# Two moves in a four-stage transformer kernel: where a tile's values are projected, and which engine issues the first stacked queries

## The chip, the cores and the metric

The kernel runs on one core of a Trainium2 chip. The metric is the device time of one execution in microseconds (us). TensorE is called PE here as in the profile, VectorE is DVE, ScalarE is ACT, GpSimd is POOL, and SyncE, which issues most transfers, is SP.

## The reference, cut to what matters

Four blocks follow one another on x of 2048 tokens by 128 channels: an attention with 16 heads of 8 channels over all 2048 keys, a feed-forward block with weights and activations rounded to blockwise FP4, a causal attention over groups of 512 tokens, and a stack of six layers. Each of the six layers is a local attention (16 heads of 64, windows of 32 keys and the window before), an output projection and a feed-forward block:

```
qkv = shift(x) @ Wqkv[i];  q, k, v = split(qkv)          # 128 -> 3 x 1024
q = rotary(l2norm(q) * q_scale);  k = rotary(l2norm(k) * k_scale)
out = softmax(8 * q k^T over the window) @ v;  x = out @ Wo[i] + x
x = (a * gelu(gate)) @ W2[i] + b2 + x,  with a, gate from layernorm(shift(x))
```

## The kernel before

**Start and first attention.** `attention_inputs` normalises x, projects and rotates queries and keys, and cuts each into three bf16 pieces, which SP writes to the DRAM tensor `pieces`. `attentions` follows, after a barrier of all engines. Its SP program loads the pieces back in stacked form: `stack_keys(0, ...)` for the first two pairs of heads (14 transfers), `stack_queries(0, ...)` for the first chunk of 512 queries (12 transfers), `stack_keys(1, ...)` for the other six pairs (14), then `stack_queries` for chunks 1 to 3 (36), then weights. A transfer of `stack_keys` writes 8 partitions with one row of 2048 bf16 elements (4096 bytes) for each pair; one of `stack_queries` writes 8 partitions with eight runs of 512 elements (1024 bytes). All of a core's queues share 16 DMA engines.

The first work of PE is `max_block` of unit 0. It waits for `stack_k[0]` and for `stack_q[0]`, so for all 14 + 12 transfers. DVE reduces each block (`reduce_block`, L914), through a ring of three PSUM banks. Unit 1 waits for `stack_k[1]`, after the 64 blocks of unit 0. Scores, exponentials on ACT and all that comes later follow from there in a fixed order.

**Layers.** `layers` runs 6 layers of 16 tiles of 128 tokens; each engine has its own written-out order of a tile's steps in `attend`, and semaphores tie them. For tile T, PE turns (transposes) the rotated queries of T (`turn` r = 0, 1), does `out_project(T - 2)`, turns the keys (r = 2, 3), projects the keys of T + 1 (`project(l, T + 1, 1, b)`), turns the weights of T - 1, computes `scores(T)` and `values(T - 1)`, projects the queries of T + 2 and last the values of T + 1. The projections of queries and keys share PSUM banks 0 and 1, so each waits until DVE has normalised the one before (`l_qn`, L1656). The values go to banks 3 and 4, which the scores use too: their projection waits for `subtract` of the tile before, and `scores(T)` waits until ACT has copied the values out (`store_values`, L1500). Of the values' copy a shifted one, `V_earlier`, is made by two transfers of SP; `values(T)` waits for them.

ACT stores the turned queries and keys (`store_qk`, L1509 to L1516), squares projected rows for the norms (L1486), moves weights and outputs, takes the exponentials, and ends a tile with `store_values(l, T + 1)`. DVE sums the squares (L1645), normalises (L1656), multiplies by cosines (L1665), and takes maxima, differences and sums of the softmax. POOL makes the sine products and `hat`, the rotated queries (L1209), which `turn` reads.

Of the kernel before, what the change touches and what calls it, by code (L numbers as in the profile page):

```python
# [17 lines left out]
CH = 512  # L18
# [6 lines left out]
HD = P // H  # L25
# [3 lines left out]
TERMS = [(0, 0), (0, 1), (0, 2), (1, 0), (1, 1), (2, 0)]  # L29
# [200 lines left out]
def attentions(nc, t, a, d):  # L230
# [33 lines left out]
    for u in range(causal, NU):  # L264
        width_before.append(width_before[-1] + sum(BLOCK_START + x[3] for x in max_blocks(u)))
    ahead = lambda u: min(start_of(causal) + (first_step[NU - 1] - first_step[causal - 1]) * width_before[u - causal]
                          // width_before[-1], first_step[u] - LEAD)
    for u in range(1, NU):
        blocks = list(enumerate(max_blocks(u)))
        at, until = start_of(u), first_step[u] - LEAD  # L270
        if u >= causal:
            at, until = ahead(u), min(ahead(u + 1) if u + 1 < NU else until, until)
# [43 lines left out]
    with ExitStack() as ctx:  # L316
# [5 lines left out]
        stack_q = [s.stack_q0, s.stack_q1, s.stack_q2, s.stack_q3]  # L322
# [3 lines left out]
        QS = sb("QS", [P, NC, H // 2, CH], BF16)  # L326
# [51 lines left out]
        with nc.Block() as block:  # L378
            @block.sync
            def _(e):  # L380
# [12 lines left out]
                def stack_queries(c, signal):  # L393
                    for odd in range(2):
                        for j in range(len(TERMS)):
                            at = 64 * odd + HD * j
                            e.dma_start(QS[at:at + HD, c, :, :],
                                        paired(d.pieces[0, TERMS[j][0]])[odd][:, :, c * CH:(c + 1) * CH])\
                                .then_inc(signal, 16)
# [44 lines left out]
                        e.dma_start(t.scales[:, 2 * i + 1, ROT:LD], v[:, 0:ROT].partition_broadcast(P)).then_inc(s.w_tab, 16)  # L444

                stack_keys(0, slice(0, 2))
                stack_queries(0, stack_q[0])
                stack_keys(1, slice(2, H // 2))
                for c in range(1, NC):
                    stack_queries(c, stack_q[c])  # L450
# [4 lines left out]
                for u, (A, c, g) in enumerate(units):  # L455
                    e.wait_ge(s.split, 2 * u + 2)
                    for j in range(2):
                        for odd in range(2):
                            at = 64 * odd + MROW + j
# [329 lines left out]

            @block.scalar  # L790
            def _(e):

                def take(use):
                    e.wait_ge(s.st_ready, place[use] + 1)
                    return 2 * pair_of[use]
# [86 lines left out]
                for u, (A, c, g) in enumerate(units):  # L882
                    for kt in range(tiles_of(u)):
                        n = first_step[u] + kt
# [192 lines left out]
def layers(nc, t, a):  # L1077
# [4 lines left out]
    with ExitStack() as ctx:  # L1082
# [47 lines left out]
        with nc.Block() as block:  # L1130
# [115 lines left out]
            def _(e):  # L1246
# [6 lines left out]
                def project(l, T, i, b):  # L1253

                    n = l * NT + T
                    if i == 0 and b == 0 and T % TC == 0:
                        e.wait_ge(s.xs, XS_START + l * SHIFTS - 2 * (NC - 1 - T // TC))
                    if i == 2 and T:
                        e.wait_ge(s.sub, START + n)
                    elif i or T:  # L1260
                        e.wait_ge(s.qn, 2 * (2 * n + i) - 1 + b)
                    if i == 0 and T < 2:
                        e.wait_ge(s.v_done, START + n)
                    at = i * INNER + b * CH
                    e.matmul(ps[:, (V_BANK[T] if i == 2 else 0) + b, :], XS[:, T * P:(T + 1) * P], w_qkv[:, at:at + CH],  # L1265
                             start=True, stop=True).then_inc(s.v_ready if i == 2 else s.a_ready, 1)

                def turn(l, T, r):

                    n = l * NT + T  # L1270
                    i = r // 2
                    e.wait_ge(s.rotated, START + (n * 2 + i) * 3 + 3)
                    if T == 0 and r == 1:
                        e.wait_ge(s.xs, XS_START + l * SHIFTS)
                    if r in (1, 2):
                        e.wait_ge(s.o_free, START + (2 * n - 4 + r if T > 1 else l * (2 * NT)))
                    else:
                        e.wait_ge(s.t_free, START + 4 * n + (1 if r else 0))
                    for j in range(4):
                        at = (4 * (r % 2) + j) * P  # L1280
                        tr = e.transpose(ps[:, TURN_BANK[r], j * P:(j + 1) * P], hat[:, i, at:at + P], t.ident[:, :])  # L1281
                    tr.then_inc(s.t_ready, 1)
# [83 lines left out]
                def attend(l):  # L1366

                    for T in range(NT):
                        ahead = T + 1 < NT
                        turn(l, T, 0)  # L1370
                        turn(l, T, 1)
                        if T >= 2:
                            out_project(l, T - 2)
                        turn(l, T, 2)
                        turn(l, T, 3)
                        if ahead:
                            project(l, T + 1, 1, 0)
                            project(l, T + 1, 1, 1)
                        if T:
                            turn_weights(l, T - 1, 0)  # L1380
                            turn_weights(l, T - 1, 1)
                        scores(l, T, 0)
                        scores(l, T, 1)
                        if T:
                            values(l, T - 1, 0)
                            values(l, T - 1, 1)
                        if T + 2 < NT:
                            project(l, T + 2, 0, 0)
                            project(l, T + 2, 0, 1)
                        if ahead:  # L1390
                            project(l, T + 1, 2, 0)
                            project(l, T + 1, 2, 1)
                    out_project(l, NT - 2)
                    mean(l, 0)
                    mean(l, 1)
                    turn_weights(l, NT - 1, 0)
                    turn_weights(l, NT - 1, 1)
                    values(l, NT - 1, 0)
                    values(l, NT - 1, 1)
                    mean(l, 2)  # L1400
                    out_project(l, NT - 1)
# [74 lines left out]
            def _(e):  # L1476
# [21 lines left out]
                def store_values(l, T):  # L1498
                    e.wait_ge(s.v_ready, START + (l * NT + T) * 2 + 2)
                    e.copy(V[:, T % 3, :], flat2(ps[:, V_BANK[T]:V_BANK[T] + 2, :])).then_inc(s.v_done, 1)  # L1500

                def store_qk(l, T, r):

                    n = l * NT + T
                    e.wait_ge(s.t_ready, START + 4 * n + r + 1)
                    j0 = 4 * (r % 2)
                    if r < 2:
                        bank = ps[:, TURN_BANK[r], :].rearrange("p (j w q) -> p j w q", j=4, q=WIN)
                        e.copy(qT[0:LD, T % 2, j0:j0 + 4, :, 0, :], bank[0:LD, :, :, :])  # L1509
                        e.copy(qT[LD:P, T % 2, j0:j0 + 4, :, 1, :], bank[LD:P, :, :, :]).then_inc(s.t_free, 1)  # L1510
                    else:
                        e.copy(kT[:, T % 2, j0:j0 + 4, WIN:WIN + P], ps[:, TURN_BANK[r], :].rearrange("p (j n) -> p j n", j=4))\
                            .then_inc(s.t_free, 1)
                    if r == 3 and T + 1 < NT:
                        e.wait_ge(s.t_free, START + 4 * n + 4)
                        e.activation(kT[:, (T + 1) % 2, :, 0:WIN], kT[:, T % 2, :, P:P + WIN], ACT.Copy,  # L1516
                                     scale=const[:, 3:4] if (T + 1) % TC == 0 else 1.0)
# [36 lines left out]
                def attend(l):  # L1554
                    for T in range(NT):
                        ahead = T + 1 < NT
                        for r in range(4):
                            store_qk(l, T, r)
                        if ahead:
                            squares(l, T + 1, 1, 0)  # L1560
                            squares(l, T + 1, 1, 1)
                        if T:
                            place_low(l, T - 1, 0)
                        if ahead:
                            inverse_norms(l, T + 1, 1)
                        if T:
                            place_low(l, T - 1, 1)
                        if T:
                            store_o(l, T - 1, 0)
                            store_o(l, T - 1, 1)  # L1570
                        if T + 2 < NT:
                            squares(l, T + 2, 0, 0)
                            squares(l, T + 2, 0, 1)
                        exponentials(l, T)
                        if T + 2 < NT:
                            inverse_norms(l, T + 2, 0)
                        if ahead:
                            store_values(l, T + 1)
                    place_low(l, NT - 1, 0)
                    place_low(l, NT - 1, 1)  # L1580
                    square_centred(l, 0)
                    square_centred(l, 1)
                    store_o(l, NT - 1, 0)
                    store_o(l, NT - 1, 1)
                    square_centred(l, 2)
# [366 lines left out]
```

## Time and profile before

| | |
|---|---|
| median of three runs | 3145.54 us (3144.41 to 3152.8) |
| profiled execution, its own time | 3135.21 us |
| span of the profiled execution | 3133.4 us |
| mean granted PE clock | 0.971 |
| PE, DVE, ACT, POOL busy | 89%, 83%, 71%, 44% of the span |

The span runs from the first to the last instruction of one execution. A busy share is a mean over stages that have different limits, so it doesn't say what a change in one stage is worth. In the timelines the idle time before an instruction and what ended it stand in brackets at the end of a row.

### The profile page before, as it was taken

To read this page: it belongs to the slowest core of one execution; us is meant where nothing else is said; L and a number is where in the kernel's file an instruction comes from. 1 tells how busy PE (TensorE), PEld (TensorE's weight loads), DVE (VectorE), ACT (ScalarE), POOL (GpSimd) and SP (SyncE) were. 2 spreads that over 40 slices of the span, in tenths; PEclk is the share of its full clock that TensorE was granted. 3 is DMA by queue.
4 is the path that set the end of the run, shared out by engine and by line. 5 is a ranking of instruction groups with operands and counts; after the bars stand their busy time and mean duration, and the time that the engine had idled before them with its cause. 6 is when DMAs were issued, how large, how long until landed. Compare 5 with 4: busy or idle time off the path is not lost. (4 is left out here: it accounts for less than half of the span.)

```text
span 3133.4 us, 74866 instructions
## 1 busy us (share of the span) xinstructions
PE 2802.7 (89%) x29085; PEld 1564.2 (50%) x29181; DVE 2594.8 (83%) x3866; ACT 2238.7 (71%) x3690; POOL 1365.0 (44%) x818
## 2 busy tenths in 40 slices
PE   3999898998898989879998998999899899999998
PEld 1233333333333333346655665666476656655764
DVE  4999889888887788469968996998699779968995
ACT  2277777767656667768867886887688778867884
POOL 0200333523335210056645664666466546646661
PEclk8699999999999999989999999999999999999999
DMA  3200001010010020011111111111111111111110
GB/s 112 69 1 2 1 8 32 1 32 8 9 32 2 21 68 2 2 39 41 36 43 43 35 35 44 42 35 57 29 35 36 57 29 35 35 50 35 39 38 21
DMA packets 62995, 101.21 MB, mean 32 GB/s; under 512 B 20450, under 2 KB 45216, under 8 KB 61472
## 3 DMA queue, kind: packets, MB, share of 16 engines
q1 hardware_dynamic: 62636, 96.26, 11.0%
q8 instruction: 245, 4.01, 0.5%
q14 instruction: 114, 0.93, 0.1%
HBM read 38.30 MB, written 7.34 MB: 15 GB/s over the span
## 5 line engine op out<-in xcount | busy, mean ns | idle before, releaser
L914 DVE TENSOR_REDUCE a_part<-ps 128x1 f32<-128x512 f32 (+3 forms) x1664 | 984.9, 652 | 157.8 <-PE ps L594 150.9
L890 ACT ACTIVATE a_Pb<-ps 128x1024 f32<-128x1024 f32 (+3 forms) x832 | 762.7, 974 | 347.8 <-PE ps L760 346.4
L1265 PE MATMUL ps<-early 128*128 128x512 f32 x1152 | 555.7, 615 | 76.7 <-DVE l_qn L1656 60.1
L1202 POOL TENSOR_TENSOR l_sine<-l_qn,stack 128x512 f32<-128x512 f32 x192 | 344.1, 1792 | 201.2 <-DVE l_qn L1656 193.5
L1226 POOL TENSOR_TENSOR l_weights<-l_weights,l_rcp 128x1024 f32<-128x1024 f32 x96 | 182.7, 1903 | 476.1 <-DVE l_rcp L1694 476.1
L594 PE MATMUL ps<-stack,a_QS 48*128 48x512 bf16 x1024 | 312.7, 405 | 72.2 <-DMA a_QS<-pieces 30.0
L1265 PEld LDWEIGHTS ps<-early 128*128 128x128 f32 x1152 | 205.0, 191 | 301.9 <-issue 144.9
L1645 DVE TENSOR_REDUCE l_norm<-l_square 128x8 f32<-128x512 f32 x384 | 252.8, 683 | 114.4 <-ACT l_square L1486 107.1
L1486 ACT ACTIVATE l_square<-ps 128x512 f32<-128x512 f32 x384 | 226.1, 594 | 89.0 <-PE ps L1265 87.8
L1665 DVE TENSOR_TENSOR l_cosine<-l_qn,stack 128x1024 f32<-128x1024 f32 x192 | 282.3, 1470 | 4.1
L644 PE MATMUL ps<-a_Pb,V 128*32 128x256 f32 (+1 forms) x3968 | 279.7, 398 | 0.0
L1656 DVE SCALAR_TENSOR_TENSOR l_qn<-l_norm,ps 128x512 f32<-128x512 f32 x384 | 246.1, 681 | 4.6 <-ACT l_norm L1496 0.2
L1203 POOL TENSOR_TENSOR l_sine<-l_qn,stack 128x512 f32<-128x512 f32 x192 | 249.5, 1299 | 0.0
L594 PEld LDWEIGHTS ps<-stack,a_QS 48*128 48x128 bf16 x1024 | 75.9, 94 | 345.1 <-DVE a_part L914 266.1
L1209 POOL TENSOR_TENSOR l_hat<-l_cosine,l_sine 128x1024 f32<-128x1024 f32 x96 | 227.5, 2370 | 21.3 <-POOL l_sine L1203 19.4
L1299 PE MATMUL ps<-l_kT,l_qT 128*64 128x64 f32 x6144 | 221.2, 225 | 14.0
L1281 PE MATMUL ps<-ident,l_hat 128*128 128x128 f32 x1536 | 207.9, 278 | 20.7 <-issue 4.9
L493 POOL TENSOR_TENSOR a_xc<-x,a_stat 128x512 f32<-128x512 f32 x12 | 12.5, 1040 | 483.8 <-DVE a_stat L971 483.8
L1299 PEld LDWEIGHTS ps<-l_kT,l_qT 128*64 128x64 f32 x6144 | 194.7, 138 | 54.1 <-issue 54.1
L1281 PEld LDWEIGHTS ps<-ident,l_hat 128*128 128x128 f32 x1536 | 176.1, 142 | 83.0 <-issue 62.9
L1345 PE MATMUL ps<-l_oT,l_w_o 128*128 128x128 f32 x1536 | 188.2, 276 | 4.1 <-ACT l_oT L1540 4.1
L1333 PE MATMUL ps<-l_wT,l_V_earlier 128*64 128x64 f32 x3072 | 185.3, 222 | 2.4 <-ACT l_wT L1532 2.4
(214 smaller groups left out, 5065.7 us busy)
## 6 DMA issues: line engine op xcount, KB each, us to landing
l_V_earlier<-l_V SPq DMA_DIRECT2D x96, 384.0 KB, 3.5
l_V_earlier<-l_V SPq DMA_DIRECT2D x96, 128.0 KB, 3.3
early<-in_L_ffn_Wqkv_dram SPq DMA_DIRECT2D x6, 1536.0 KB, 8.3
a_QS<-pieces SPq DMA_DIRECT2D x96, 64.0 KB
pieces<-a_piece SPq DMA_DIRECT2D x6, 512.0 KB, 2.6
pieces<-early SPq DMA_DIRECT2D x12, 256.0 KB, 2.7
a_KS<-pieces SPq DMA_DIRECT2D x48, 64.0 KB
l_w_o<-in_L_ffn_Wo_dram SPq DMA_DIRECT2D x6, 512.0 KB, 4.0
```

The source lines that it names most:

```text
L594: mm = e.matmul(bank[:, 0:width], QS[rows, c, pair, qt * P:(qt + 1) * P], KS[A][rows, pair, b * CH:b * CH + width], start=not masked, stop ...
L644: mm = e.matmul(O[32 * h:32 * h + 32, lo:hi], V[A][:, kt, at:at + 32], Pb[:, n % 2, h, lo:hi], start=(kt == 0), stop=(kt == tiles_of(u) - ...
L890: e.activation(Pb[:, n % 2, 2 * p:2 * p + 2, lo:CH], ps[:, 2 * p:2 * p + 2, lo:CH], ACT.Exp)\
L914: e.tensor_reduce(part[:, u % 2, column(h, qt), b:b + 1], bank[:, 0:width], AX.X, ALU.max)\
L1202: e.tensor_tensor(sine[:, :, 0:ROT], swap[:, :, ROT:LD], table[:, :, 0:ROT], ALU.mult).then_inc(s.rotated, 1)
L1203: e.tensor_tensor(sine[:, :, ROT:LD], swap[:, :, 0:ROT], table[:, :, ROT:LD], ALU.mult).then_inc(s.rotated, 1)
L1265: e.matmul(ps[:, (V_BANK[T] if i == 2 else 0) + b, :], XS[:, T * P:(T + 1) * P], w_qkv[:, at:at + CH], start=True, stop=True).then_inc(s.v ...
L1281: tr = e.transpose(ps[:, TURN_BANK[r], j * P:(j + 1) * P], hat[:, i, at:at + P], t.ident[:, :])
L1299: mm = e.matmul(ps[half:half + LD, bank, at:at + LD], qT[:, T % 2, j, w, :, :], kT[:, T % 2, j, WIN * w:WIN * (w + 2)], start=False, stop= ...
L1645: e.tensor_reduce(norm[:, 0, heads], square[:, heads, :], AX.X, ALU.add).then_inc(s.total, 1)
L1656: e.scalar_tensor_tensor(out=qn[:, i, heads, :], in0=norm[:, 2, heads].unsqueeze(2).to_broadcast([P, HALF, LD]), scalar=1.0 / NORM_MIN, in ...
L1665: e.tensor_tensor(cosine[:, i, :, :], qn[:, i, :, :], tab[:, 2 * i, T, :].unsqueeze(1).to_broadcast([P, LH, LD]), ALU.mult).then_inc(s.cos ...
```

## The change

Two edits that have nothing to do with each other.

- In `attentions` the 12 transfers of `stack_queries(0)` leave SP's order, where they stood between the two groups of keys, and stand first in ACT's program. Addresses, sizes and the semaphore stay.
- In `attend` of `layers` PE projects the values of tile T (T > 0) inside tile T, behind the two turns of its queries, and no longer at the end of tile T - 1. ACT copies them out between the stores of the queries and those of the keys. The values of tile 0 stay where they are.

```diff
                 stack_keys(0, slice(0, 2))
-                stack_queries(0, stack_q[0])
                 stack_keys(1, slice(2, H // 2))
...
             def _(e):
+                for odd in range(2):
+                    by_pair = d.pieces[0].rearrange("t (h p d) n -> t p d h n", p=2, d=HD)
+                    for j in range(len(TERMS)):
+                        at = 64 * odd + HD * j
+                        e.dma_start(QS[at:at + HD, 0, :, :], by_pair[TERMS[j][0], odd][:, :, 0:CH]).then_inc(stack_q[0], 16)
...
                         turn(l, T, 0)
                         turn(l, T, 1)
+                        if T:
+                            project(l, T, 2, 0)
+                            project(l, T, 2, 1)
                         if T >= 2:
                             out_project(l, T - 2)
...
                             project(l, T + 2, 0, 0)
                             project(l, T + 2, 0, 1)
-                        if ahead:
-                            project(l, T + 1, 2, 0)
-                            project(l, T + 1, 2, 1)
...
-                        for r in range(4):
+                        for r in range(2):
+                            store_qk(l, T, r)
+                        if T:
+                            store_values(l, T)
+                        for r in range(2, 4):
                             store_qk(l, T, r)
...
-                        if ahead:
-                            store_values(l, T + 1)
```

## Rows read from the trace of the kernel before

**Rows 1.** Page, part 1: busy time and instructions of each engine.

```profile
PE 2802.7 (89%) x29085; PEld 1564.2 (50%) x29181; DVE 2594.8 (83%) x3866; ACT 2238.7 (71%) x3690; POOL 1365.0 (44%) x818
```

**Rows 2.** Timeline of the start, all engines: start, us, what.

```profile
62.39 2.04 SPq L388 DMA_DIRECT2D stack<-pieces  x6
...
67.10 4.10 SPq L397 DMA_DIRECT2D a_QS<-pieces  x12
71.24 2.13 SPq L388 DMA_DIRECT2D stack<-pieces  x6
...
75.93 1.01 PE L594 MATMUL ps<-stack,a_QS 48*128 48x512 bf16 x3 [29.99 <-DMA a_QS<-pieces]
...
76.55 33.57 DVE L914 TENSOR_REDUCE a_part<-ps 128x1 f32<-128x512 f32 x56 [19.11 <-PE ps L594]
```

**Rows 3.** Transfers at 63.3 to 69.3 us; the share is of 16 DMA engines.

```profile
DMA packets 330, 0.83 MB, mean 138 GB/s; under 512 B 99, under 2 KB 141, under 8 KB 327
...
q1 hardware_dynamic: 330, 0.83, 49.1%
```

**Rows 4.** Transfers at 80 to 95 us.

```profile
DMA packets 394, 1.44 MB, mean 96 GB/s; under 512 B 57, under 2 KB 57, under 8 KB 390
...
q1 hardware_dynamic: 392, 1.41, 51.0%
```

**Rows 5.** Transfers at 106 to 111 us.

```profile
DMA packets 997, 0.91 MB, mean 181 GB/s; under 512 B 112, under 2 KB 997, under 8 KB 997
...
q1 hardware_dynamic: 997, 0.91, 53.0%
```

**Rows 6.** Timeline of SP's queue at 80 to 82 us.

```profile
77.27 9.12 SPq L397 DMA_DIRECT2D a_QS<-pieces  x1
```

**Rows 7.** Transfers at 92.5 to 93.3 us, by queue.

```profile
q14 instruction: 1, 0.01, 4.3%
```

**Rows 8.** Timeline of a tile in the middle of a layer, all engines.

```profile
2002.28 1.99 PE L1265 MATMUL ps<-early 128*128 128x512 f32 x4 [0.67 <-DVE l_qn L1656]
...
2007.24 2.38 POOL L1209 TENSOR_TENSOR l_hat<-l_cosine,l_sine 128x1024 f32<-128x1024 f32 x1 [0.24 <-POOL l_sine L1203]
...
2009.64 3.71 PE L1265 MATMUL ps<-early 128*128 128x512 f32 x8
2009.66 1.23 DVE L1685 TENSOR_TENSOR l_weights<-ps,l_nmax 128x1024 f32<-128x1024 f32 x1
...
2011.04 0.19 PEld L1265 LDWEIGHTS ps<-early 128*128 128x128 f32 x1 [0.24 <-DVE l_weights L1685]
...
2011.53 1.45 DVE L1645 TENSOR_REDUCE l_norm<-l_square 128x8 f32<-128x512 f32 x2 [0.65 <-ACT l_square L1486]
...
2013.18 1.03 PE L1281 MATMUL ps<-ident,l_hat 128*128 128x128 f32 x8
...
2014.16 0.99 ACT L1500 COPY l_V<-ps 128x1024 f32<-128x1024 f32 x1
...
2016.86 1.28 DVE L1656 SCALAR_TENSOR_TENSOR l_qn<-l_norm,ps 128x512 f32<-128x512 f32 x2
...
2017.45 1.07 ACT L1512 COPY l_kT<-ps 128x512 f32<-128x512 f32 x2
...
2017.60 1.99 PE L1265 MATMUL ps<-early 128*128 128x512 f32 x4 [0.67 <-DVE l_qn L1656]
```

**Rows 9.** Timeline of tile 0 of the first layer.

```profile
1374.51 1.99 PE L1265 MATMUL ps<-early 128*128 128x512 f32 x4 [1.00 <-DVE l_weights L1685]
...
1378.19 1.14 PE L1281 MATMUL ps<-ident,l_hat 128*128 128x128 f32 x8 [0.82 <-DVE l_hat L1673]
```

**Rows 10.** Timeline of PE in tiles 14 and 15 of the first layer.

```profile
1588.16 1.99 PE L1265 MATMUL ps<-early 128*128 128x512 f32 x4 [1.23 <-DVE l_weights L1685]
...
1595.34 1.09 PE L1314 MATMUL ps<-ident,l_weights 128*128 128x128 f32 x8 [1.66 <-POOL l_weights L1226]
```

**Rows 11.** Busy time by stretch: the six layers.

```profile
1340.00:3133.00 1793.00, 1646.81 (x17924) 1126.70 (x18019) 1494.48 (x1924) 1372.02 (x2675) 1038.00 (x601) 0.99 0.13 39
```

## Prediction

> **What bounds the kernel now.** I read the page's busy shares first, then the timeline of the start and of one tile of a layer, then the transfers by stretch, and last the ends of a layer. PE is the busiest engine [rows 1], and in the six layers it is busy 1646.8 of 1793 us [rows 11], so both edits have to be judged by what PE waits for.
>
> At the start PE waits 29.99 us, and the wait ends with the stacked queries; its first score block is at 75.93 [rows 2]. SP issues the keys of two pairs from 62.39, the 12 transfers of queries from 67.10 to 71.20, and the other keys from 71.24 [rows 2]. From 76.55 DVE sets the pace with 56 reductions in 33.57 us, 0.60 each [rows 2]. The later work follows from these blocks in a fixed order, so the time at which PE starts is passed on whole to the end.
>
> In a layer one tile takes 2017.60 - 2002.28 = 15.32 us, from one projection of keys to the next [rows 8]. What repeats is a loop of two engines. PE may project keys when DVE has normalised the queries before; the projection of the next queries starts at 2009.64; ACT squares them; DVE, which has waited 0.65 for the squares, starts its sums at 2011.53, does cosines, an addition and the softmax sums, and normalises at 2016.86; then PE, which has waited 0.67, projects the next keys at 2017.60 [rows 8]. PE's part of the loop runs from 2002.28 to the end of the first query projection, the rest of it from there to 2017.60 is DVE's. The reader should see that the values' projection stands in the second stretch: the row at 2009.64 holds 8 records, of which four are the queries and four, from 2011.04, the values [rows 8]. PE is off the loop there, and has 0.67 to spare.
>
> **Edit 2, the values in the layers.** The projection keeps its cost. Its four records begin at 2011.04 and the turns at 2013.18 follow on it; one record takes (2013.18 - 2009.64)/8 = 0.44, so the values take 1.8 and the turns of queries, which now come first, start at about 2011.4 instead of 2013.2 [rows 8]. What they need is `hat`, which POOL finishes at 2007.24 + 2.38 = 2009.62, 1.8 ahead of the earlier start [rows 8]. The values' wait for the difference of the tile before ends at 2009.66 + 1.23 = 2010.89, before they start even now [rows 8]. Output projection, turns of keys and the projection of keys come after the same sum of PE work, so they stand where they stood: 0.
>
> On ACT the copy of the values starts at 2014.16 and the stores of keys at 2017.45; the copy and the four stores of queries fill the 3.29 between without a gap [rows 8]. In the new order the stores of queries begin at 2014.16, the copy follows at about 2016.6, and the stores of keys again at 2017.45: 0. The scores wait for the copy and for the stores of keys, and the latter stay last. The two transfers of `V_earlier` are issued some 2.4 us later, but their reader comes a whole tile (15.32) later, so they are hidden; without that cover each late microsecond would be 96 in the whole. Behind ACT's copy stand the keys' stores and the squares of keys; they would be late only if the values came after 2016.6, and PE ends them at about 2014.
>
> Before tile 1 PE waits 1.00 for DVE's difference ahead of the values, but after the turns of queries it waits 0.82 again for DVE's `hat` of the keys [rows 9]. Turning queries first fills the first wait and lengthens the second; DVE's chain isn't touched: 0. Before tile 15 it waits 1.23 for DVE and, a few steps on, 1.66 for POOL's weights [rows 10]: the same, 0. So the sum for this edit is 0 for 96 tiles. Its bounds: a gain would have to come out of the 0.67 that PE waits, 96 x 0.67 = 64 us at most, but that wait ends with DVE, whose work doesn't depend on the values; a loss begins when `hat` comes more than 1.8 later. I take 0, with 1 us either way for changed neighbours on PE.
>
> **Edit 1, the stacked queries.** SP's order loses 12 issues, 4.10 us [rows 2], and ACT, idle until the first scores, has the same 12 to issue, beside the first keys. No row shows ACT issuing a transfer. If issuing were the limit, everything would be issued at 67.1 instead of 71.2 and PE would start up to 4.1 earlier. But the transfers themselves are the limit. In the first stretch 186 packets of 4 KB and 42 of 1 KB keep 49.1% of 16 engines busy, so about 8 engines, all the time [rows 3]; in the stretch of the other keys it is 337 packets of 4 KB at 51.0% [rows 4]; in a stretch of queries alone 885 of 1 KB at 53.0% [rows 5]. From these a 1 KB packet costs 5 x 16 x 0.53/885 = 0.048 of an engine, a 4 KB one of the other keys 15 x 16 x 0.51/337 = 0.363, and one of the first keys (6 x 16 x 0.491 - 42 x 0.048)/186 = 0.24. SP's queue runs full: one issue is held 9.12 us at 77.27 [rows 6]. So half of the engines are the only ones at work, and never idle; a second issuer brings no bandwidth.
>
> What changes is the order. Before, the first keys, then the first queries, then the other keys went through one queue, and each of the 8 engines had 24 x 0.24 + 96 x 0.048 = 10.4 us of work ahead of PE's start (12 transfers x 2 rows, and 12 x 8 runs). The other keys, 12 x 6 = 72 rows an engine at 0.363, or 26.1 us, stood behind. After, SP issues these other keys right behind the first ones, from 67.1, while ACT's queue still holds queries. The two queues now compete, and the one with 4 KB packets has the heavier ones. If an engine takes a packet from each in turn, 24 queries have gone when the 24 first keys have, at 63.3 + 24 x (0.24 + 0.048) = 70.2; the other 72 queries alternate with the 72 rows of the other keys: 72 x (0.363 + 0.048) = 29.6, so the last lands at 99.8, not 75.9: +23.9. If the small packets fit into gaps of the large ones, it is 63.3 + 5.8 + 26.1 = 95.2, +19.3. If the queries get two packets for one in the first stretch, 48 remain: 71.4 + 48 x 0.411 = 91.1, +15.2. I take +21.
>
> That an engine does turn to another queue while SP's is full, a row shows: a packet of the instruction queue passes at 92.5 to 93.3 [rows 7]. That it does so after one packet, not after a whole transfer, the row doesn't show; this is the open point of the forecast.
>
> The Trainium skill (DMA: Bandwidth & Descriptors, Queues, rings and completion order) says that an engine drains a whole packet, typically 9 to 17 descriptors, from one queue before it takes the next. If what it calls a packet is one transfer's share of an engine, this speaks for the first rival below, and the sum would be about 0; no row here shows how large a turn is. The same page (Issuing engines are not separate DMA queues) says that a second issuer saves the issue time alone, and by this the sum would be at best 4.1 off.
>
> **Sum.** The profiled execution: span 3133.4, own time 3135.2; +21 + 0 gives 3156. The median of the three runs stands 10.3 above that execution, so against the median it is 3145.5 + 21 = 3166.5. From no change a measurement here can tell about 0.3%, 9.4 us.
>
> **The rivals.**
>
> *Turns by whole transfers (not slower).* An engine takes a transfer's share from each queue: 8 runs, 0.38, against 2 rows, 0.48. After 12 of each, 63.3 + 12 x 0.86 = 73.7, both groups are through, the same 10.4 of work as before, and the other keys have not come between. PE starts at 75.9 or, with the issue time saved, up to 4.1 earlier; I take -1: 3144.5. For it: the sum of work ahead is the same, and nothing in a row excludes it. Against it: it needs that the heavier packets are not served one by one. It decides once fewer than some 23 of the other keys' rows (9.4/0.411) go before the last query.
>
> *Other engines for ACT's queue.* If ACT's transfers went to the idle half, the queries would be there with the first keys, at about 70: -5.6, so 3140. Against it: a transfer has the same shape whoever issues it, and half of the engines serve every stretch [rows 3 to 5].
>
> *The queries' turn becomes the wait.* If POOL's `hat` is later than 1.8 + 0.67 = 2.5 us in most tiles, every further 0.1 costs 96 x 0.1 = 9.6: 3155 without edit 1. Against it: 1.8 of slack in each tile.
>
> *The layers gain.* If the earlier stores of queries shorten the loop by 0.1 or more a tile, it is 9.6 less: 3136. Against it: neither engine of the loop waits for them.
>
> **How the numbers follow.** Turns by packets 0.56, by transfers 0.33, other engines 0.05, the turn waits 0.03, the layers gain 0.03. Predicted is the first, 3166.5. Its own range is +15 to +24 with 2 for the runs' spread and the layers: 3159 to 3172. The whole range has to reach the second case, whose chance is over 2 in 10: 3141 to 3172. Faster by over 0.3%: 0.03. Within: 0.33 + 0.05 = 0.38. Slower: 0.56 + 0.03 = 0.59.
>
> **What would show it.** In the new trace PE's first score block should stand between 91 and 100 and its wait should end with the queries; ACT should show 12 issues from 62.4; the stretch from 70 to 90 should hold both 4 KB and 1 KB packets in near equal number, at half of the engines. A first block at 75 with the 1 KB packets all gone by then shows the second case; a share well over half shows the third. In the layers the turn of queries should follow the query projection directly, and the tile should still take 15.32, with PE waiting 0.67 for `l_qn`. The prediction is wrong if PE starts by 80, or if the tile's time moves by 0.1.

## The result, and the profile after

The changed kernel takes 3169.92 us (median of 20 runs, 3149.47 to 3186.84) beside 3144.70 for the kernel before (20 runs): ratio 1.0077, interval 1.0058 to 1.0096, or 25 us more (18 to 30). It is slower by more than 0.3%, as forecast, and the forecast 3166.5 lies 3.4 under it. One of the 20 executions of the kernel before took 11443.69 and isn't explained; without it that median is 3144.42. The profiled execution has a span of 3184.7 and an own time of 3186.5; it is one of the longest of the 20, 16.6 above their median.

Page of the changed kernel, part 1, beside [rows 1], and two queues of part 3:

```profile
PE 2840.7 (89%) x29181; PEld 1577.8 (50%) x29181; DVE 2596.9 (82%) x3866; ACT 2239.3 (70%) x3690; POOL 1365.1 (43%) x818
...
q1 hardware_dynamic: 61772, 95.48, 11.0%
...
q10 hardware_dynamic: 864, 0.79, 0.1%
```

PE's busy time grew by 38, but with it 96 records that are missing in [rows 1] (29085 there); this row alone shows no more work. New is queue q10, which carries ACT's 12 transfers.

Timeline of its start, beside [rows 2]:

```profile
62.22 2.02 SPq L388 DMA_DIRECT2D stack<-pieces  x6
62.23 4.46 ACTq L796 DMA_DIRECT2D a_QS<-pieces  x12
...
69.50 7.93 SPq L388 DMA_DIRECT2D stack<-pieces  x6
...
96.53 1.01 PE L593 MATMUL ps<-stack,a_QS 48*128 48x512 bf16 x3 [50.77 <-DMA a_QS<-pieces]
97.14 38.36 DVE L919 TENSOR_REDUCE a_part<-ps 128x1 f32<-128x512 f32 x64 [39.88 <-PE ps L593]
142.40 1.46 PE L759 MATMUL ps<-a_QS,stack 50*128 50x512 bf16 x4
```

ACT issues all 12 from 62.23 on, 4.9 us before SP did. Still the wait that these transfers end grew from 29.99 to 50.77, and PE's first score block moved from 75.93 to 96.53, by 20.6; DVE's 0.60 a block is unchanged. The first block of L759 (L760 in the kernel before) needs the row maxima; it moved by 18.8. Before, it had waited 1.17 for the transfers of the maxima:

```profile
123.56 1.04 PE L760 MATMUL ps<-a_QS,stack 50*128 50x512 bf16 x4 [1.17 <-DMA a_QS<-a_mrow]
```

Transfers of the changed kernel: first at 63.3 to 69.3 (beside [rows 3]), then at 80 to 89, which is in the stretch of [rows 4]:

```profile
DMA packets 297, 0.45 MB, mean 74 GB/s; under 512 B 48, under 2 KB 235, under 8 KB 297
...
q1 hardware_dynamic: 89, 0.25, 32.6%
q10 hardware_dynamic: 208, 0.19, 21.2%
```

```profile
DMA packets 353, 0.79 MB, mean 87 GB/s; under 512 B 41, under 2 KB 201, under 8 KB 353
q1 hardware_dynamic: 176, 0.62, 40.6%
q10 hardware_dynamic: 177, 0.16, 11.2%
```

At 80 to 89 the other keys (q1, 4 KB) and the queries (q10, 1 KB) pass packet for packet: 176 and 177. The counts hold 4-byte packets too, eight for each transfer (q10's 864 on the page are 12 x 64 and 12 x 8), 41 of them under 512 B here; without them it is 353 - 201 = 152 of 4 KB to 201 - 41 = 160 of 1 KB. The shares add up to 51.8% of 16 engines, half of them again. Reckoned as in the forecast, on the packets that carry data, one of q1 costs 9 x 16 x 0.406/152 = 0.385 of an engine, one of q10 9 x 16 x 0.112/160 = 0.10, a pair 0.49; the forecast had 0.363, 0.048 and 0.411. In the first stretch it is otherwise: 235 - 48 = 187 packets of queries to 297 - 235 = 62 of keys, three to one. A packet of queries costs 6 x 16 x 0.212/187 = 0.11, one of the first keys 6 x 16 x 0.326/62 = 0.50, where [rows 3] gave 0.048 and 0.24. Only 74 GB/s pass instead of 138. A part of this is the mix, since more of the packets are small; by the costs of [rows 3] and [rows 5] the same packets would have taken 62 x 0.24 + 187 x 0.048 = 24 us of an engine, and they took 6 x 16 x 0.538 = 52.

Timeline of a tile of a layer, beside [rows 8]:

```profile
2053.75 1.99 PE L1270 MATMUL ps<-early 128*128 128x512 f32 x4
...
2055.58 1.04 PE L1286 MATMUL ps<-ident,l_hat 128*128 128x128 f32 x8
...
2055.64 1.45 DVE L1652 TENSOR_REDUCE l_norm<-l_square 128x8 f32<-128x512 f32 x2 [0.65 <-ACT l_square L1491]
...
2056.45 1.88 PE L1270 MATMUL ps<-early 128*128 128x512 f32 x4
...
2058.17 1.95 PE L1350 MATMUL ps<-l_oT,l_w_o 128*128 128x128 f32 x16
...
2061.72 1.99 PE L1270 MATMUL ps<-early 128*128 128x512 f32 x4 [0.72 <-DVE l_qn L1663]
...
2069.07 1.99 PE L1270 MATMUL ps<-early 128*128 128x512 f32 x4
```

The turns (2055.58) stand right behind the queries' projection and the values (2056.45) behind the turns. From one projection of queries to the next it is 2069.07 - 2053.75 = 15.32, as before; DVE's wait is 0.65 as before, PE's 0.72 for 0.67.

The last tile of a layer is not as before. PE in the second layer's last tile of the changed kernel, first the timeline, then the busy time by stretch (the column behind POOL is the granted clock, then the DMA share):

```profile
1934.17 1.35 PE L1319 MATMUL ps<-ident,l_weights 128*128 128x128 f32 x8 [2.30 <-POOL l_weights L1231]
...
1942.03 2.05 PE L1350 MATMUL ps<-l_oT,l_w_o 128*128 128x128 f32 x16 [0.68 <-ACT l_oT L1545]
```

```profile
1934.00:1938.00 4.00, 3.83 (x42) 2.99 (x42) 0.69 (x1) 1.74 (x3) 0.04 (x1) 0.61 0.98 328
```

The same two steps in the third layer of the kernel before, and the stretch over them:

```profile
2186.72 1.09 PE L1314 MATMUL ps<-ident,l_weights 128*128 128x128 f32 x8 [1.66 <-POOL l_weights L1226]
...
2193.06 2.05 PE L1345 MATMUL ps<-l_oT,l_w_o 128*128 128x128 f32 x16 [0.69 <-ACT l_oT L1540]
```

```profile
2187.00:2191.00 4.00, 3.85 (x97) 3.39 (x98) 1.14 (x2) 1.74 (x3) 0.00 (x0) 1.00 0.87 322
```

Before, PE waited 1.23 ahead of the values and 1.66 ahead of the turns of weights [rows 10]. With the values pulled forward the first wait is gone and the second is 2.30. In this last tile, behind the wait, the granted clock is 0.61 over 4 us, so part of these matmuls ran at the lower level (1.2 GHz), and the step from the weights' turns to the output projection takes 7.86 us for 6.34.

### The profile page after: what moved, and what is told of

It is laid out like the page before. It is cut to its first block and busy times, and to the rows that moved or that the text cites. A ratio compares the mean times of both kernels' runs of the same rounds, so it can differ in the third digit from the quotient of the medians.

```text
span 3184.7 us, 74962 instructions
## 1 busy us (share of the span) xinstructions
PE 2840.7 (89%) x29181; PEld 1577.8 (50%) x29181; DVE 2596.9 (82%) x3866; ACT 2239.3 (70%) x3690; POOL 1365.1 (43%) x818
## 5 line engine op out<-in xcount | busy, mean ns | idle before, releaser
L1270 PE MATMUL ps<-early 128*128 128x512 f32 x1152 | 573.1, 620 | 69.1 <-DVE l_qn L1663 64.4
L593 PE MATMUL ps<-stack,a_QS 48*128 48x512 bf16 x1024 | 315.3, 409 | 92.1 <-DMA a_QS<-pieces 50.8
L593 PEld LDWEIGHTS ps<-stack,a_QS 48*128 48x128 bf16 x1024 | 76.2, 94 | 367.4 <-DVE a_part L919 267.9
L1350 PEld LDWEIGHTS ps<-l_oT,l_w_o 128*128 128x128 f32 x1536 | 185.3, 191 | 49.1 <-issue 40.5
```

The costliest lines, as they stand in the source:

```text
L593: mm = e.matmul(bank[:, 0:width], QS[rows, c, pair, qt * P:(qt + 1) * P], KS[A][rows, pair, b * CH:b * CH + width], start=not masked, stop ...
L1350: mm = e.matmul(ps[:, Y_BANK, 0:P], w_o[:, j, :], oT[:, j, :], start=(j == 0), stop=(j == PAIRS - 1))
```

## The experiments

"Wait" below is the time from the first issue of keys to PE's first score block, since the first issue itself lies between 59.8 and 62.5 from kernel to kernel. With the start as it was, five profiles give 12.9 to 18.7: the kernel before 75.93 - 62.39 = 13.5 and, once more, 75.42 - 62.50 = 12.9; the three kernels below that have edit 2 or a part of it alone 74.31 - 60.31 = 14.0, 79.34 - 62.17 = 17.2 and 78.91 - 60.24 = 18.7. The changed kernel has 96.53 - 62.22 = 34.3.

**The two edits alone.**

```
# edit 1 alone: the line leaves SP's program, the twelve issues go to ACT's
-                stack_queries(0, stack_q[0])
# edit 2 alone
+                        if T:
+                            project(l, T, 2, 0)
+                            project(l, T, 2, 1)
...
-                        if ahead:
-                            project(l, T + 1, 2, 0)
-                            project(l, T + 1, 2, 1)
```

> Edit 1 alone. Theory A (the whole loss is the late start: two queues take turns on half of the engines): PE's first score block at about 96, as in the changed kernel, and the time +17 to +21 us over before. Rival B (a part of the +25 us comes from the values in the layers): clearly less than +25 here, and the second attempt, edit 2 alone, makes up the rest. Rival C (the late start lets PE's granted clock fall more often, which costs more than the start itself): the start is +20, the time about +25, and the extra appears in the attentions before 1340 us, with the clock below that of before.

> Edit 2 alone. Theory A and rival C: no change within 0.3%, a tile of a layer still takes 15.32 us, PE waits 0.67 for the normalised queries, and the copy of the values stands behind the four stores of queries. Rival B (the layers lose through edit 2): +3 to +8 us, with the six layers longer than their 1793 us of before.

Edit 1 alone: 3156.74 beside 3143.43, ratio 1.0041 (1.0019 to 1.0063), 13 us (6 to 20). Its wait is 91.95 - 60.18 = 31.8:

```profile
60.18 2.02 SPq L388 DMA_DIRECT2D stack<-pieces  x6
...
91.95 1.01 PE L593 MATMUL ps<-stack,a_QS 48*128 48x512 bf16 x3 [48.24 <-DMA a_QS<-pieces]
```

Edit 2 alone: 3152.88 beside the same 3143.43, ratio 1.0019 (0.9995 to 1.0043): 6 us more that can't be told from none. So edit 1 is by the medians the larger part, and turns by whole transfers, which gave no loss and a start of PE at 75.9 or earlier, are refuted by the wait. The start of the second kernel, where nothing was edited, had the longest wait of its kind, 78.91 - 60.24 = 18.7. So some 5 us of a start come and go by the execution, and the transfers show where. Here are those of this kernel at 61.2 to 67.2, the same stretch behind the first issue as in [rows 3]:

```profile
DMA packets 172, 0.48 MB, mean 81 GB/s; under 512 B 56, under 2 KB 56, under 8 KB 170
q1 hardware_dynamic: 172, 0.48, 51.4%
```

With SP's queue alone, 172 - 56 = 116 packets cost 6 x 16 x 0.514/116 = 0.43 each, not 0.24. In the same way the other profiles with one queue give 0.23 and 0.24 where the wait was 12.9 and 14.0, and 0.39 where it was 17.2. The 0.24 on which the forecast rests was one draw of several, and the dear packets of the changed kernel's first stretch are not shown to come from the second queue.

In the second kernel too the lower clock came in last tiles:

```profile
2201.97 1.42 PE L1314 MATMUL ps<-ident,l_weights 128*128 128x128 f32 x8 [2.30 <-POOL l_weights L1226]
...
2209.83 2.05 PE L1345 MATMUL ps<-l_oT,l_w_o 128*128 128x128 f32 x16 [0.69 <-ACT l_oT L1540]
```

**Who competes: the other keys held back, and the other keys on ACT.** The first kernel is edit 1 with SP waiting for the queries before it issues the other keys; the second leaves the queries on SP and gives ACT the other keys.

```
# other keys held back
-                stack_queries(0, stack_q[0])
+                e.wait_ge(stack_q[0], 16 * 2 * len(TERMS))
                 stack_keys(1, slice(2, H // 2))
# other keys on ACT: SP's line goes, ACT issues the same transfers
-                stack_keys(1, slice(2, H // 2))
```

> Edit 1, but SP issues the other keys only when the first queries have landed, so that they can't take turns with them. If the other keys are the whole cause: PE's first score block back at 74 to 76. If mixing the two queues slows the packets by itself (in the changed kernel the first keys landed 9 us later too, with about 0.46 of an engine for a 4 KB packet and 0.11 for one of 1 KB): about 82. If ACT's queue is simply slow: still above 90.

> The order of before, but ACT issues the other keys (12 transfers of 6 rows and the ones) and SP the first keys and then the first queries. If an engine takes one packet from each queue in turn, SP's 24 + 96 packets an engine meet ACT's 72 heavy ones, all of which go first: PE's first score block at 96 to 103. If ACT's queue is served after SP's, or gets the smaller part: 76 to 80, and edit 1 was slow because it put the queries on the weaker queue. If turns go by whole transfers: 24 of SP's against 12 of ACT's, the latter all gone before: about 96 too, so this run tells the weak queue from the others, not packets from transfers.

Measured, once each: 3168.07 and 3178.15, both above all 23 executions of the kernel before in that session (3124.75 to 3163.40). PE's first block in the timeline of the kernel with the other keys held back:

```profile
84.50 1.01 PE L594 MATMUL ps<-stack,a_QS 48*128 48x512 bf16 x3 [38.61 <-DMA a_QS<-pieces]
```

And the kernel with the other keys on ACT:

```profile
62.21 2.25 SPq L388 DMA_DIRECT2D stack<-pieces  x6
62.22 2.49 ACTq L796 DMA_DIRECT2D stack<-pieces  x6
...
106.33 1.00 PE L593 MATMUL ps<-stack,a_QS 48*128 48x512 bf16 x3 [60.57 <-DMA a_QS<-pieces]
```

With the other keys held back the wait is 84.50 - 62.35 = 22.1. So of the 13 to 21 us that edit 1 adds (31.8 and 34.3 less 12.9 to 18.7), some 10 to 12 (31.8 and 34.3 less 22.1) come from the other keys, and some 3 to 9 (22.1 less 12.9 to 18.7) remain while only the first keys and the queries are under way in two queues, which do no more work than one. Whether the second queue or the draw of the packets' cost makes these 3 to 9, one execution can't tell.

Holding back is no remedy, as the same profile shows further on. SP's whole program stands behind the held keys, and the transfers of the row maxima come last in it, so PE waits once more:

```profile
134.55 2.86 SPq L460 DMA_DIRECT2D a_QS<-a_mrow  x4
...
142.24 1.04 PE L760 MATMUL ps<-a_QS,stack 50*128 50x512 bf16 x4 [11.27 <-DMA a_QS<-a_mrow]
```

This block comes 142.24 - 62.35 = 79.9 after the first issue, in the changed kernel 142.40 - 62.22 = 80.2, and in the kernel before 123.56 - 62.39 = 61.2.

With the other keys on ACT the wait is 106.33 - 62.21 = 44.1, the longest of all, although the queries' own queue and engine are those of before. So ACT's queue is not a weak one; what counts is that the other keys are under way in a second queue. In its stretch of 89 to 95 the other keys, now q10, and the queries, now q1, again pass packet for packet, 303 - 172 = 131 that carry keys to 172 - 39 = 133:

```profile
DMA packets 303, 0.67 MB, mean 112 GB/s; under 512 B 39, under 2 KB 172, under 8 KB 303
...
q10 hardware_dynamic: 152, 0.54, 41.1%
q1 hardware_dynamic: 151, 0.14, 10.6%
```

**How large a turn is: half rows.** Edit 1, with the other keys in 24 transfers of 2 KB packets instead of 12 of 4 KB. It tells turns by packets (a turn of the keys becomes cheaper) from turns by bytes (it would not).

```
+                            for half in (slice(0, N // 2), slice(N // 2, N)):
+                                e.dma_start(KS[0][at:at + HD, pairs, half], paired(d.pieces[1, TERMS[j][1]])[odd][:, pairs, half])\
```

> Edit 1 alone, with the other keys in 24 transfers of half rows (2 KB a packet) in place of 12 of whole rows (4 KB). Measured from the block's start PE waited 32 to 34 us with whole rows, some 19 of them after the first keys had landed. If an engine takes one packet from each queue in turn, each turn of the keys is now half as long, the same number of queries is over in fewer bytes of keys: the wait falls to about 24 to 29. If the engines share by bytes, or a whole transfer's share at a time weighs by its bytes: 31 to 35, no change.

3151.63, once (3147.46 for the kernel before in that session); the wait is 90.04 - 62.20 = 27.8, 4 to 6.5 shorter than with full rows. Transfers at 80 to 86 us:

```profile
DMA packets 460, 0.62 MB, mean 103 GB/s; under 512 B 56, under 2 KB 259, under 8 KB 460
q1 hardware_dynamic: 233, 0.41, 36.2%
q10 hardware_dynamic: 227, 0.21, 18.8%
```

Again 233 to 227, one for one (201 to 203 that carry data), though the keys' packets are half as large and cost 6 x 16 x 0.362/201 = 0.17. The queries pass 227 packets in these 6 us, and 177 in 9 us with full rows: 38 and 20 per us. Turns by bytes would have changed the ratio of the counts, and by whole transfers the queries would have led 8 to 6. Equal counts alone would also come of turns of two or three packets. The single records of the traces decide: if each packet is paired with one that starts within 0.03 us of its end, the second is of the other queue in 283 of 324 pairs at 80 to 89 in the changed kernel, in 368 of 443 here and in 274 of 293 with the other keys on ACT. Turns of two would give half. The turn is one packet in these stretches. In the first stretch it is not, as the next kernels help to see.

**The first queries in two parts.** If the small packets are what suffers, let few of them count: PE's first blocks need pairs 0 and 1 alone. In one kernel ACT issues these and SP the rest behind the other keys, in the other SP issues both.

```
# on SP
-                stack_queries(0, stack_q[0])
+                stack_queries(0, stack_q[0], slice(0, 2))
                 stack_keys(1, slice(2, H // 2))
+                stack_queries(0, stack_k[1], slice(2, H // 2))
```

> ACT issues only what unit 0 needs of the first queries, two pairs of heads (a quarter of the packets), beside the first keys; the other six pairs follow the other keys on SP. If only the number of packets in the competition matters: PE waits 8 to 10 us from the block's start, 3 to 5 less than before the change. If mixing two queues slows the packets by itself, as with the held keys (22 us against 13.5): about 13 to 18.

> The same split of the first queries, but all of it on SP in the order of the kernel before: first keys, the two pairs of queries, other keys, the other six pairs. No two queues. The transfers ahead of PE fall from 24 x 0.24 + 96 x 0.048 = 10.4 to 6.9 us of an engine, but the 26 issues stay 8.8 us: PE waits 10 to 11 us from the block's start, 3 less than before. Time 0 to -3 us, not to be told from no change in the median; the wait in the profile decides. Rival: the issues of 12 further transfers delay the other keys or the mrow transfers, then +2 to +4.

The first gave 3138.87, once, and a wait of 74.19 - 59.83 = 14.4, and its releaser is another: the keys' row of ones, no longer the queries. The expectation had 8 to 10 if only the number of competing packets mattered, and 13 to 18 if not.

```profile
74.19 1.03 PE L598 MATMUL ps<-stack,a_QS 48*128 48x512 bf16 x3 [30.83 <-DMA stack<-in_c_ones_dram]
```

Its transfers at 60.7 to 66.7, again the stretch that [rows 3] have behind the first issue:

```profile
DMA packets 300, 0.53 MB, mean 88 GB/s; under 512 B 97, under 2 KB 199, under 8 KB 298
q1 hardware_dynamic: 149, 0.42, 43.3%
q10 hardware_dynamic: 151, 0.10, 10.3%
```

Here 199 - 97 = 102 packets of queries pass beside 300 - 199 = 101 of larger ones, one to one, where a transfer gives an engine 2 runs of queries beside 2 rows of keys. Where it is 8 runs beside 2 rows the same stretch has 187 to 62 in the changed kernel, 220 to 65 with edit 1 alone and 192 to 49 with the other keys held back, so 3.0 to 3.9 to one. In this first stretch the counts follow the transfers' shares, roughly as the rival of turns by whole transfers would have them; only later do the packets alternate. What ends the one and begins the other no run shows.

The second, in five rounds, 3141.94 beside 3147.46, ratio 0.9981 (0.9960 to 1.0002), with a wait of 76.60 - 61.95 = 14.7. The expectation of 10 to 11 was missed: its sum took 0.24 for a packet of the first keys, and here it was 0.36. Both waits lie within those of the unedited start, 12.9 to 18.7. A gain of up to 0.4% is not excluded, and none is shown. So two queues did no visible harm once the small packets had little to send, and nothing tried here beats the kernel before for certain.

**The last tile.** To see whether edit 2's cost lies in the last tile, it is made everywhere but there, and there alone.

```
# all but the last tile
+                        if 0 < T < NT - 1:
+                            project(l, T, 2, 0)
+                            project(l, T, 2, 1)
# the last tile alone
+                        if T == NT - 1:
+                            project(l, T, 2, 0)
+                            project(l, T, 2, 1)
```

> Edit 2 alone, but the values of a layer's last tile are projected where they were. Theory D (edit 2 costs by the last tile: it joins PE's waits of 1.23 and 1.66 us into one of 2.30, after which PE's granted clock is at its lower level for the weights' turns and the scores): the wait of 2.30 is gone, the six layers last what they did before, median within 3 us of before. Rival (the moved values cost in the middle tiles or at tile 1): +6 to +9 as with edit 2 alone.

> Edit 2 in a layer's last tile alone; the other tiles and the start as before. Theory D (the joined wait of 2.30 us in the last tile is the whole cost of edit 2): the wait of 2.30 before the turns of weights in every layer, PE's granted clock below 1 behind it in most layers, the step from the weights' turns to the output projection 7.9 us instead of 6.3 where it is, and a median as with edit 2 alone, +5 to +10. Rival (the other tiles carry the cost, or the difference was chance): the wait is there, but the clock stays at 1 or the median within 3 us of before.

> The kernel before once more, for a second profile of its start. The transfers ahead of PE took 13.5 us from the block's start in the first profile, and 14.0 and 18.7 in two kernels with the same start. If the spread belongs to the transfers, this one lies between 13 and 19 too, and edit 1 costs 13 to 21 us by the execution; the late start of the changed kernel (34.3) and of edit 1 alone (31.8) lie outside it in any case.

Ratios 1.0009 (0.9991 to 1.0028) for all but the last and 1.0014 (0.9994 to 1.0035) for the last alone; the medians can't tell them apart. The kernel before once more gave 3142.26. The rows can tell them apart. The kernel with all but the last tile changed:

```profile
2188.04 1.09 PE L1314 MATMUL ps<-ident,l_weights 128*128 128x128 f32 x8 [1.68 <-POOL l_weights L1226]
...
2194.39 1.83 PE L1345 MATMUL ps<-l_oT,l_w_o 128*128 128x128 f32 x14 [0.69 <-ACT l_oT L1543]
```

And the kernel with the last tile alone, in two of its layers:

```profile
2191.44 1.09 PE L1314 MATMUL ps<-ident,l_weights 128*128 128x128 f32 x8 [2.31 <-POOL l_weights L1226]
...
2197.78 2.05 PE L1345 MATMUL ps<-l_oT,l_w_o 128*128 128x128 f32 x16 [0.69 <-ACT l_oT L1543]
...
2486.54 1.16 PE L1314 MATMUL ps<-ident,l_weights 128*128 128x128 f32 x8 [2.31 <-POOL l_weights L1226]
...
2494.35 1.83 PE L1345 MATMUL ps<-l_oT,l_w_o 128*128 128x128 f32 x14 [0.69 <-ACT l_oT L1543]
```

The same wait of 2.31 was followed by 6.34 in one layer and by 7.81 in another. Over the first five layers, counted in this way:

| kernels | wait before the weights' turns | last tiles | of them with 7.8 for 6.34 |
|---|---|---|---|
| changed kernel, edit 2 alone, last tile alone | 2.30 to 2.31 | 15 | 9 (4, 3, 2) |
| before (twice), edit 1 alone, queries in two on SP, all but the last tile | 1.65 to 1.68 | 25 | 0 |

In the sixth layer the first three show the lower clock there too. Such a step is 1.5 longer, so this execution of the changed kernel has 5 x 1.5 = 7.5 of it. But it is not all net. From the first layer's last tile to the fifth's, the three take 1184.7 to 1185.0; the other five, 1180.6 to 1184.0 with a mean of 1182.1, because another dip of the clock, some 65 to 80 us behind the last tile, comes and goes in all of them. From one last tile to the next it is 296.6 to 296.8 in the six cases that begin with the lower clock, but also in three of these kernels' six others 296.5 to 296.7, and in eight of the twenty of the other five kernels 296.3 to 296.6; the rest take 294.6 to 295.3. And the changed kernel with three such tiles in the stretch took 1184.7, the last tile alone with one of them 1185.0. The difference of the means, 2.7 and 1.5 for the sixth layer, gives an estimate of some 4 us for edit 2; that the lower clock behind the joined wait is what costs them is not shown.

## Why the prediction was right, and where it was not

**Transfers bound the start, not their issue: right.** In the changed kernel the issues came 4.9 us earlier and PE 20.6 later, again at half of the 16 engines (51.8% with two queues, 51.0% in [rows 4]). That refutes the rival of other engines for ACT's queue.

**The other keys get between: right, one packet in turn.** This was the open point, with 0.33 for turns by whole transfers. The counts of 176 to 177, 152 to 151 and, with half-size packets, 233 to 227, and the order of the single records, settle it for the stretch in which the other keys and the queries compete. While the first keys are under way the rival's rule is the nearer one (3.0 to 3.9 packets of queries to one of keys, with shares of 8 and 2), but the rival needed it to hold to the end. The Trainium skill (DMA: Bandwidth & Descriptors, Queues, rings and completion order) has whole packets of typically 9 to 17 descriptors drained before the engine turns; if such a packet is a transfer's share of an engine, the counts of the later stretch speak against it and those of the first, roughly, for it.

**First keys through at 70.2: wrong.** This step took the packet costs of one queue at a time, from one execution, and a strict alternation. By the records of the changed kernel the last of the 192 packets of first keys ended at 77.2, and 484 of the 768 packets of queries had passed by then, not 192. Measured in the first stretch are 0.50 and 0.11 instead of 0.24 and 0.048. The two errors have opposite signs: the keys were later, but more queries had gone meanwhile. The remaining 284, 35.5 an engine, at 0.49 a pair give 77.2 + 17.4 = 94.6; the last one ended at 94.9, near the forecast 75.9 + 21 = 96.9 all the same. The kernel that holds the other keys back shows the first part by itself: a wait of 22.1, where the sum of packet costs allowed 10.4 behind 63.3, as in the kernel before. The forecast of +21 was met in the profile (+20.6), in part by luck: through two errors that cancelled, and a forecast of 21 chosen between sums of 15.2 and 23.9.

**Passed on whole to the end: nearly.** Of the 20.6, 18.8 are left at the first block that needs the maxima. By the waits, edit 1 adds 33.0 (mean of 31.8 and 34.3) less 15.3 (mean of 12.9, 13.5, 14.0, 17.2 and 18.7), which is 17.8, less the 1.8 absorbed: 16; its own runs gave 13 (6 to 20).

**Edit 2 at 0 in 96 tiles: right for the steady tiles, wrong for the last.** The order, the 15.32, the 0.65 and PE's wait came out as forecast, and neither the rival in which the queries' turn becomes the wait nor a gain appeared. The step that didn't hold is "Before tile 15 ... the same, 0". The two waits were seen and named [rows 10], and their sum even fell; what was not weighed is that the clock may be lower after one wait of 2.30 where it stayed up after 1.66, for up to 1.5 x 6 = 9 us. What it costs net the profiles put at some 4, an estimate that the medians (6 for edit 2 alone, which can't be told from none) neither confirm nor exclude.

**The sum.** 16 + 4 = 20, beside 25 measured (18 to 30), where the 4 is not shown. The profiled execution of the changed kernel stands 51.3 above that of before, and these terms don't fill that. The largest other part is the attention stage of L593 and L759. First the kernel before, then the changed one, by stretch:

```profile
110.00:1370.00 1260.00, 1117.45 (x11097) 426.46 (x11097) 1046.10 (x1882) 862.70 (x1031) 342.09 (x223) 0.96 0.07 16
```

```profile
131.00:1414.00 1283.00, 1137.07 (x11118) 432.38 (x11119) 1048.82 (x1883) 864.34 (x1035) 342.32 (x224) 0.93 0.07 15
```

The same work (11097 and 11118 matmuls) took some 23 us more at a granted clock of 0.93 for 0.96. Edit 1 alone had 0.95 there. Across the 20 runs of the changed kernel the span goes from 3147.7 at a mean clock of 0.969 to 3185.1 at 0.956, with a correlation of -0.96, so most of this is the draw of one execution. A small part may belong to the edits: the mean clock over the 20 runs is 0.961, beside 0.967 over 23 of the kernel before in the first session of experiments. PE's wait at the start counts in it at 0.50, so 20.6 us more of it take 0.003; some 0.002 is left, and at 2650 us of span for 1 of clock (the slope over the 20 runs) that is an estimate of 5 us, about what the sum lacks. No run shows which edit, if any, it comes from. Open too are why the first stretch mixes the queues by another rule than the later one, and why a packet of the first keys costs 0.24 in one execution and 0.43 in another.

## What to carry to other kernels

In these runs transfers that share the same DMA engines kept their order only inside one queue. Moving an urgent one to a second queue frees it from the issuer and exposes it to everything behind it: where the engines take packets in turn, as in the later stretch here, an urgent transfer of small packets gets one small packet through for each large one of its rival. Before such a move, multiply the urgent packets on an engine by the cost of a pair, and look whether the engines, not the issuer, are full. Take the costs from more than one execution. And a wait in the issuer's program holds back all that stands behind it: look where the next wait moves.

When a stage's order is changed, look at its last pass separately, and at the longest single wait of PE, not only at the sum of waits: here two waits joined to one were followed by the lower clock in most cases, though their sum fell.

## What was not expected of the hardware

- The same transfers of first keys, in the same order and in one queue, cost 0.23 to 0.43 of an engine a packet by the execution, and PE's start moved by up to 5.8 us with it. With a second queue beside them they cost 0.50 in the changed kernel and 6 x 16 x 0.294/65 = 0.43 with edit 1 alone (at 61.1 to 67.1), so how much of it the second queue adds stays open.
- Two hardware queues that both had work passed one packet each in turn, whatever the packets' size (4 KB or 2 KB against 1 KB) and whichever engine had issued them, once the first keys were through. While these were under way the counts followed the transfers' shares of an engine: 3.0 to 3.9 to one with 8 runs beside 2 rows, one to one with 2 beside 2. Why it changes no run shows.
- A wait of 2.30 us, with about the same matmuls ahead of it, was followed by the lower clock in 9 of 15 cases and not in the other 6; one of 1.66 in none of 25.
- The granted clock differs from run to run of one kernel enough (0.955 to 0.969) to move its time by 1.2%, so a profile of one execution can't carry a difference of less.
